# One product a block and head in a tiled decayed scan, sums of squares on ScalarE, and a new order of work

## What is computed

```python
def reference(x, ...):                        # x: (16, 120000)
    h = _L0_tok_ref(x)                        # frames of 128 samples, 938 a row, orthonormal DCT
    h = h + _L0_attn_ref(_layernorm(h), ...)  # decayed linear attention, then an MLP 128-512-128
    h = h + _L0_ffn_ref(_layernorm(h), ...)   # one of 8 experts (by position) 128-512-128
    return h

# inside _L0_attn_ref, 4 heads of 32 columns:
    q = jnp.exp(rmsnorm(q, rms_scale)); k = jnp.exp(rmsnorm(k, rms_scale))
    def step(carry, inp):
        A, z = carry
        qt, kt, vt = inp
        A = lam[None, :, :, None] * A + kt[..., None] * vt[..., None, :]
        z = lam[None] * z + kt
        St = jnp.einsum('bhi,bhij->bhj', qt, A)
        Zt = jnp.einsum('bhi,bhi->bh', qt, z)
        return ((A, z), (St, Zt))
    att = (S / Zs[..., None]).reshape(Bx, Tx, Cx)
    att = g * att @ Wo.T
...
```

## Time and profile before

| | us |
|---|---|
| time, median of 3 runs | 1027.73 |
| lowest, highest | 1026.53, 1029.47 |
| time of the profiled execution | 1025.9 |
| its span, first to last instruction | 1024.1 |
| TensorE busy in it | 985.9 (96%) |
| VectorE busy | 851.6 (83%) |
| ScalarE busy | 655.8 (64%) |
| GpSimd busy | 343.2 (34%) |

### The profile page before, as it was taken

One profiled execution on the slowest core, in us unless ns is written; L12 is line 12 of the kernel. 1 busy time (PEld: TensorE's weight loads), 2 busy tenths in 40 slices (PEclk: granted clock), 3 DMA queues, 4 the chain that ended last, 5 costly groups with the idle time before them and its releaser, 6 DMA issues.

```text
span 1024.1 us, 47082 instructions
## 1 busy us (share of the span) xinstructions
PE 985.9 (96%) x20067; PEld 746.1 (73%) x20067; DVE 851.6 (83%) x2690; ACT 655.8 (64%) x1240; POOL 343.2 (34%) x175
## 2 busy tenths in 40 slices
PE   6669999999999999999999999999999999999987
PEld 5567777787777778777777777777777767877654
DVE  6979888888988888898888988888898888889632
ACT  3337565766756667675766857576685757667553
POOL 5232335243233523333342233424323342432310
PEclk9879999999999999999999999999999999999999
DMA  5442425143332414324242341524234151413310
GB/s 176 150 130 70 106 62 145 44 128 86 96 97 74 124 56 114 107 66 128 74 115 66 103 118 53 140 64 119 71 102 119 46 148 58 124 54 99 104 31 19
DMA packets 71631, 96.95 MB, mean 95 GB/s; under 512 B 11360, under 2 KB 46720, under 8 KB 71424
## 3 DMA queue, kind: packets, MB, share of 16 engines
q1 hardware_dynamic: 71424, 93.94, 33.1%
HBM read 27.89 MB, written 10.83 MB: 38 GB/s over the span
## 4 chain that ended last, share of the span: by engine, by line
PE 94%; DVE 2%; DMA 1%; ACT 1%; issue 1%; POOL 0%; SPq 0%; DVEq 0%; ACTq 0%; POOLq 0%
PE bank L1004 14%; PE bank L1149 11%; PE bank L1171 11%; PE bank L1142 10%; PE bank L1009 10%; PE bank L1177 10%; PE bank L1087 8%; PE bank L1082 4%; PE bank L1119 3%; PE bank L1126 3%; PE bank L1165 2%; PE bank L1035 2%; PE bank L1077 2%; PE bank L1059 1%; PE bank L1048 1%
## 5 line engine op out<-in xcount | busy, mean ns | idle before, releaser
L605 ACT ACTIVATE hid<-bank,f1b 128x512 f32<-128x512 f32 (+1 forms) x128 | 81.8, 653 | 139.2 <-PE bank L1171 138.8
L452 POOL TENSOR_TENSOR t_sum<-x,hs 128x512 f32<-128x512 f32 x32 | 40.7, 1273 | 361.9 <-DVE x L832 337.9
L1087 PE MATMUL bank<-qx,ki 128*32 128x16 f32 x7680 | 127.1, 192 | 4.7 <-issue 4.7
L1149 PEld LDWEIGHTS bank<-w,hid 128*128 128x128 f32 x1024 | 118.0, 192 | 8.7 <-issue 7.2
L456 POOL TENSOR_TENSOR rr<-vv,nhalf 128x8 f32<-128x8 f32 x32 | 78.4, 2449 | 136.0 <-DVE vv L713 136.0
L1149 PE MATMUL bank<-w,hid 128*128 128x128 f32 x1024 | 119.6, 275 | 0.8 <-ACT hid L585 0.8
L1171 PE MATMUL bank<-xa,f1w 128*128 128x512 f32 (+1 forms) x256 | 118.0, 576 | 1.0 <-issue 0.9
L1142 PE MATMUL bank<-c,w 128*128 128x512 f32 (+1 forms) x256 | 117.0, 570 | 0.9 <-ACT c L579 0.9
L441 POOL TENSOR_TENSOR ab<-af,heads 128x1792 f32<-128x1792 f32 x16 | 78.7, 4916 | 114.9 <-DVE af L813 114.9
L1087 PEld LDWEIGHTS bank<-qx,ki 128*32 128x32 f32 x7680 | 112.0, 110 | 5.1 <-issue 4.9
L1177 PE MATMUL bank<-hid,f2w 128*128 128x512 f32 (+1 forms) x256 | 107.6, 563 | 0.6 <-issue 0.6
(11 more groups left out here) (139 smaller groups left out, 2242.7 us busy)
## 6 DMA issues: line engine op xcount, KB each, us to landing
qx<-qq SPq DMA_DIRECT2D x256, 80.0 KB, 2.9
hs<-hs SPq DMA_DIRECT2D x32, 532.0 KB, 4.9
v<-v_f SPq DMA_DIRECT2D x32, 256.0 KB
zq<-rz_dram SPq DMA_DIRECT2D x64, 128.0 KB
gz<-gate_f SPq DMA_DIRECT2D x16, 512.0 KB, 3.1
xT<-in_xT SPq DMA_DIRECT2D x16, 468.5 KB, 3.5
f1w<-in_fc1T SPq DMA_DIRECT2D x16, 256.0 KB, 2.7
f2w<-g_dram SPq DMA_DIRECT2D x16, 256.0 KB, 3.3
```

The costliest lines, as they stand in the source:

```text
L605: nc.scalar.activation(hid[:, j, cols(g)], bk(f"f1_{g}{j}")[:, 0:width[g]], ACT.Gelu, bias=f1b[:, b % E, j:j + 1]).then_inc(ge2, 1)
L1087: return mm(D[r, :, t + j:t + WIN:EIGHT], ki[:, j, s0:s0 + WIN], x[:, :, t0 + j:t0 + WIN:EIGHT], start=True, stop=True)
L1149: last = mm(dst[:, P * i:P * i + P], hid[:, j, P * m:P * m + P], w2[:, j, :], start=(j == 0), stop=(j == 3))
```

## The change

The scan: the state's rows of a head (32) are put under the values of a block (64 rows) in `sx`, and the rows of `qc` under the weights in `px`, so that one product a block and head, over 128 rows of which 96 are in use, gives both parts. `px` becomes a ring of four (`RING`), with a tile for each of the two blocks. `qc` goes to DRAM (`rows_out`) and back by head into `px` (`rows_back`, one DMA a block); `hand_sx` copies the values to `sx`; `states` now copies the decayed sums to `sx` and stands on ACT. `heads1` and `ab` go, `hs1` moves to DRAM. The sums of squares are an output of the squaring on ACT, one instruction a tile instead of one for four; `sums` on DVE goes. All five lists of steps and the lists of banks are in a new order.

```diff
+RING = 4
 USES = [
-    [("w1_01", 3), ("v0", 2), ("n2T1", 3), ...
+    [("qT1", 2), ("w1_03", 3), ("zt", 2), ("w2_1", 3), ("f1_01", 3), ("f2_0", 3), ("f1_10", 3), ("f1_13", 3), ("k1", 1)],
+    [("n2T0", 3), ("v1", 2), ("w1_02", 3), ("dct0", 1), ("w1_12", 3), ("n1T0", 3), ("nT1", 1), ("f1_03", 3), ("n1T1", 3), ("oT0", 3), ("f1_12", 3), ("k0", 1), ("oT1", 3)],
...
+    [("w1_00", 3), ("u", 2), ("at0", 3), ("at1", 3), ("f1_11", 3), ("wo0", 2), ("f2_1", 3), ("g0", 1)],
...
-        ab = sb("ab", NST, P)
-        px = [sb(f"px{i}", HEADS, BLK) for i in range(2)]
+        sx = [sb("sx0", TILES, P), sb("sx1", TILES, P)]
+        px = [[sb(f"px{i}{o}", HEADS, BLK) for o in (0, 1)] for i in range(RING)]
...
+        key_rows = [slice(0, BLK), slice(BLK, P)]
+        state_rows = [slice(BLK, BLK + HD), slice(0, HD)]
...
+            def rows_out(b):
+                for i in range(RING):
+                    before(sp, row_in[i], b, ring_rows[i], ring_rows[i])
+                sp.wait_ge(qc_ok, nth(b, 1, 1))
+                sp.dma_start(qc_dram[:, :], qc[:, 0:NBLK * BLK]).then_inc(qcd_in, 16)
+
+            def rows_back(b, c):
+                sp.wait_ge(qcd_in, nth(b, 16, 16))
+                ring_free(sp, b, c)
+                for o in range(blocks[c]):
+                    t = BLK * (2 * c + o)
+                    sp.dma_start(px[c % RING][o][state_rows[o], :, :],
+                                 qc_dram[:, t:t + BLK].rearrange("(h d) n -> d h n", h=HEADS)).then_inc(row_in[c % RING], 16)
...
             def body(at):      # SP, a round in the new order
                 if (b := at(2)) is not None:
+                    rows_back(b, 2); rows_back(b, 0); rows_back(b, 3); rows_back(b, 1); spread(b, 2); hand_gate(b)
+                    rows_back(b, 7); rows_back(b, 4); spread(b, 3)
...
+                if (b := at(1)) is not None:
+                    spread(b, 1); hand_v(b); rz_out(b); hand_sx(b); rz_back(b); rows_out(b); hand_h2(b)
...
             def squares(b, i, g):
-                nc.scalar.activation(qk[i][:, four(g), :], by_tile(bk(f"{name}{g}")[:, :]), ACT.Square).then_inc((sq_ok, sk_ok)[i], 1)
+                for j, m in enumerate(tiles(g)):
+                    last = nc.scalar.activation(qk[i][:, m, :], src[:, j, :], ACT.Square, accum_out=ssq[:, i, m:m + 1])
...
+            def states(b):     # on ACT
+                for o in (0, 1):
+                    for hd in range(HEADS):
+                        r = slice(HD * hd, HD * hd + HD)
+                        src = af[r, :].rearrange("p (e c) -> p c e", e=HD)[:, 1 - o::2, :]
+                        last = nc.scalar.activation(sx[o][state_rows[o], 1 - o:KT + 1 - o, r], src, ACT.Copy)
...
+                for o in range(blocks[c]):     # pxs, and merge in the same way
+                    r = key_rows[o]
+                    last = nc.scalar.activation(px[c % RING][o][r, :, :], between_of(c)[r, :, :], ACT.Copy)
...
             def body(at):      # ACT, part of a round
+                if (b := at(2)) is not None:
+                    attn_in(b)
+                if (b := at(3)) is not None:
+                    gelu2(b, 1, 0)
                 if (b := at(1)) is not None:
                     squares(b, 0, 0); squares(b, 0, 1)
+                if (b := at(3)) is not None:
+                    gelu2(b, 1, 1)
+                if (b := at(2)) is not None:
+                    pxs(b, 4)
+                if (b := at(3)) is not None:
+                    gelu2(b, 1, 2); gelu2(b, 1, 3)
...
             def scan(b, c):
-                        for hd in range(HEADS):
-                            mm(S[r, t:t + BLK], ab[:, i - 1, r], qc[:, BLK * i:BLK * i + BLK], start=not opened, stop=False, skip_group_check=True)
+                pe.wait_ge(row_in[ring], nth(b, ring_rows[ring], ring_rows[ring] if c >= RING else 16 * blocks[c]))
                 pe.wait_ge(px_ok, nth(b, TILES, c + 1))
-                        last = mm(S[r, t:t + BLK], v[:, o, c, r], px[c % 2][:, hd, :], start=False, stop=True, skip_group_check=True)
+                        last = mm(S[r, t:t + BLK], sx[o][:, c, r], px[ring][o][:, hd, :], start=True, stop=True)
...
             def body(at):      # PE, the new order of a round (numbers: element's stage)
+                3: n2T0  2: g1  3: scan5 scan6 scan7  2: qT1 kT1 v1  3: w1_00 attends1 w1_01 w1_02 w1_03
+                2: pairs0  3: w2_0  2: pairs1 zt  1: dct0  3: n2T1  1: dct1  2: u  3: w1_10 to w1_13
+                2: pairs2  3: n1T0 nmT0 w2_1 at0  2: pairs3  1: nT0 nT1  3: f1_00 to f1_03 f2_0 nmT1 n1T1
+                2: scan0 scan1 scan2  3: at1 oT0  1: q0 q1  3: f1_10 f1_11  2: scan3 pairs4  3: f1_12 f1_13
+                2: attends0  1: k0 k1  2: scan4 pairs5  3: f2_1  1: qT0  2: pairs6  1: g0  3: oT1  1: v0
+                2: pairs7  1: kT0
```

332 lines of the change are left out of this document (173 added, 159 removed), and 7 rows, old and new, of the table USES.

## The result

The changed kernel takes 1048.97 us (median of 4 runs, 1046.69 to 1057.01), the kernel before 1027.36 us beside it: a ratio of 1.0227, 95% interval 1.0198 to 1.0255. It is slower, and outside the predicted range. The profiled execution is the longest of the four, 1057.01 us, with a span of 1055.2 us; the kernel before had 1024.1.

A forecast was written before the change was run, and what follows sets the result against it. PE (TensorE), busy 96% of the span, was taken to bound the kernel. From the 1024.1 us span, -24.9 (products), +5.7 (ACT stand) and +1.5 (ends) gave 1006.4, plus 1.8 and 1.8 made 1010.0 us; range 1001 to 1024.

The forecast's parts named there:

- POOL: "all off the path": POOL loses the states copies; its 20.8 us of busy time at most a round all lie off the path, costing nothing.
- four rivals: Alternatives: dear sums out of ACT (0.11), late rows (0.10), later landings of the rows (0.05), a late DVE hand-over (0.05).
- rival 3: Scan rows queue behind the large hs2 copy and land 4.1 us late a round: 1071 us, chance 0.05.
- What leaves PE, 24.9 us: Scan on PE: 1792 state products (L1119) go, at 14 ns each, 1.56 us an element, 24.9 us in all.
- The 25 ns: The Trainium skill's least start-to-start time of a matmul; would give back 45 us, near 990 us; given no part in the sum.
- ACT, +5.7 us: ACT's squares make PE stand 0.38 us a round ahead of k0, over fifteen steady rounds 5.7 us.
- s: Time of one 128x128 square with its sum on ACT: 0.16 to 0.48 us, taken as 0.33.
- 8s - 2.26: PE's stand (idle wait) a round at k0 in us: nothing at s = 0.18, 0.38 at 0.33, 1.58 at 0.48.
- DVE, nothing: DVE's sums go (-2.4 us), split merges come (+2.3); every hand-over to PE ahead of its need, so no cost.
- SP and the rows, hidden with 3 us to spare: qc's way through DRAM into px for scan 1 takes some 21 to 26.5 us against 24.4 of PE work; taken as hidden.
- The ends, +1.5 us: Start and end of the run: memsets 3.5 us, squares about 1, less gaps the new order fills; -2 to +5, taken +1.5.
- The round: Steady round length: 58.8 us by PE alone, w2s(0) starting every 58.8 to 59.3 us.

The follow-up runs named there:

- e1: The changed kernel with store(3, 0) moved ahead of rows_back(7), rows_back(4) and spread(3) in SP's list: 1019.16 us, ratio 0.9924.
- e16: The kernel before without the 112 state products an element (L1119) and without 8 pair products an element: 1007.15 us, ratio 0.9804.
- e4: e1 with every scan product issued twice: 1039.81 us, ratio 1.0129.
- e9: The kernel before with only the 112 state products an element (L1119) left out: 1025.39 us, ratio 0.9994.
- e8: e1 without the 240 copies of the rows into px and their waits: 1015.49 us, ratio 0.9888.
- e6: The kernel before with ACT's squares giving their own sums and DVE's sums gone: 1028.84 us, ratio 1.0022.
- e5: e1 with the clearing of px moved behind the first variance1 and that of sx behind the first normed: 1014.89 us, ratio 0.9883.
- e12: The changed kernel with e10's place of the store and e5's moved memsets together: 1013.97 us, ratio 0.9873.
- e10: The changed kernel with store(3, 0) behind rows_back(7) and rows_back(4) but ahead of spread(3): 1015.08 us, ratio 0.9887.
- e17: e12 with satisfied semaphore waits put into PE's list, nine ahead of each wide product, to bring its packets in step: 1023.55 us, ratio 0.9975.
- e18: e12 with 10 pair products an element left out to hold its packets in step: 1012.5 us, ratio 0.9856.
- e3: The changed kernel with the store early and both norms' powers ahead of the residual in POOL's list: 1029.5 us, ratio 1.0028.

## Why the prediction was wrong, step by step

- **POOL: "all off the path".** This is the step that failed. POOL's busy time is off the path; its list is not. The text named `rows_back(4)` and `spread(3)` as queued behind the wait for scan 3 and stopped there: the next entry of SP's list is `store(3, 0)`, for which POOL's `resid` waits, and with it `powq(1)`, DVE's tokens and PE. It cost 29.8 us (e1 against the changed kernel). None of the four rivals has it; rival 3 has its size (over 1.2 us a round) but another mechanism, and PE waited for the rows of `px` 0.5 us in all, once.
- **What leaves PE, 24.9 us.** The mechanism was right, the term was mis-sized. 14 ns is how far apart these products start; leaving them out gives 9.6 ns each (e16) and doubling them 10.8 (e4), 17 to 19 us. And it gives that only if the round stays in step with the instruction packets, otherwise nothing (e9). The 25 ns that the prediction also names (45 us) are far off here: the largest price measured is 10.8.
- **ACT, +5.7 us.** s is 0.25 us, from the starts of squares in a row (487.50, 487.75, 488.00 us in e1; the accumulator read lies under the next square), not 0.33. The step's own formula, 8s - 2.26, then gives no stand at k0, and none is seen. The states cost 4.7 us a round on ACT (eight of 0.59), where the sum had 2.6; ACT shows 47.7 us of a round and that, too, was covered. Table loads fell from 60 to 30, as forecast.
- **DVE, nothing.** Right: with the store early PE waits for DVE in no middle round.
- **SP and the rows, hidden with 3 us to spare.** Right: landing took 2.0 us (median), and PE waits for rows only in the first element; the copies cost about 3.7 us at most (e8).
- **The ends, +1.5 us.** Too low. In e1 the first `w2` comes 9.1 us later than before, the last step is 3.2 us and the end 0.6 us shorter: +5.3 us. The forecast had 3.5 us for the memsets and 1 for the squares, and took 3 back for gaps that the new order would fill. The squares alone put the first `w2` 2.2 us later (e6). The memsets are 3.6 us of it by e5 against e1 and 0.5 by e12 (95.6 us) against e10 (96.0), so their size stays open. And in e1's fill PE waits 4.2 us for the first element's rows of `px`, in two waits, where the kernel before waited 3.0 us for DVE's `px`.
- **The round.** Forecast 59.2 us with the stand; measured 59.1 to 59.4 in the undisturbed rounds of e1. That is right by two errors against each other: 0.4 us of a stand that isn't there, and 0.4 us of products that give less.

With the store and memsets mended the sum nearly comes out, in part by luck, since the stand that isn't there makes up for most of what the products give less: e12 takes 1014 us, the forecast was 1010. The open part is the spread of its rounds (58.7 to 60.9 us), which look like e9's, but which e17 and e18 failed to tie to the packets. Open too: why e10 is faster than e1, and why a product left out is worth 9.6 ns and not the 14 at which it starts.

## What to carry to other kernels

When a list of a queue is reordered, follow every entry behind a new wait, down to the last one before the list's next wait, through the engine that waits for it and that engine's own list; busy time says nothing of it. Look, too, at which instructions of VectorE and GpSimd the new order lets run at the same time (e3). Look for the slack (here under 2.4 us) and put a store, whose landing frees a buffer, ahead of loads that aren't due. And a TensorE-bound kernel of many small products has a second clock: before crediting a removed instruction, compare the places of the instruction packets in a round, and repeat the measurement with the stream shifted.
